# Second attention: the probability transpose moved from TensorE to DMA transposes of fp16 halves

## The reference

```python
q = _rope(_rms_norm((draft_hidden @ Wq.T).reshape(bsz, draft_len, H, HD), q_norm_w))
k = _rope(_rms_norm((kv_in @ Wk.T).reshape(bsz, total_len, KVH, HD), k_norm_w))
v = (kv_in @ Wv.T).reshape(bsz, total_len, KVH, HD)
scores = jnp.einsum('bhqd,bhkd->bhqk', q, k) * SCALE
probs = jax.nn.softmax(scores, axis=-1)
attn = jnp.einsum('bhqk,bhkd->bhqd', probs, v)
return attn.reshape(bsz, draft_len, H * HD) @ Wo.T
```

## Time and profile before

| | us |
|---|---|
| median of 3 runs | 3430.97 (3428.15 to 3434.47) |
| profiled execution | 3434.46 |
| its span | 3432.7 |
| second attention in it | 2141 to 2983 |

### The profile page before, as it was taken

One profiled execution on the slowest core, in us unless ns is written; L12 is line 12 of the kernel. 1 busy time (PEld: TensorE's weight loads), 2 busy tenths in 40 slices (PEclk: granted clock), 3 DMA queues, 4 the chain that ended last, 5 costly groups with the idle time before them and its releaser, 6 DMA issues. The chain is left out here.

```text
span 3432.7 us, 59039 instructions
## 1 busy us (share of the span) xinstructions
PE 3004.1 (88%) x17256; PEld 1779.6 (52%) x17257; DVE 1807.7 (53%) x5546; ACT 1647.5 (48%) x4343; POOL 1697.2 (49%) x2331
## 2 busy tenths in 40 slices
PE   4899999999999529999999997799999999743996
PEld 2566666665665415555555543455555555432663
DVE  4455555555555235434334444688788778521331
ACT  5777777876876213333322332455555555321332
POOL 6666666666663354454534453544444444142222
PEclk9899999999999569999999998999999999856998
DMA  6211011011010254455544565000000000117444
GB/s 234 84 53 40 31 53 40 31 53 40 31 50 31 94 198 132 143 156 153 145 141 138 153 182 140 17 21 23 18 24 18 24 18 13 50 67 287 86 84 104
DMA packets 206771, 291.78 MB, mean 85 GB/s; under 512 B 39200, under 2 KB 110368, under 8 KB 206624
## 3 DMA queue, kind: packets, MB, share of 16 engines
q1 hardware_dynamic: 143824, 211.36, 18.8%
q0 software_dynamic: 16640, 38.05, 5.5%
q10 hardware_dynamic: 46224, 41.36, 4.1%
HBM read 199.27 MB, written 95.63 MB: 86 GB/s over the span
## 5 line engine op out<-in xcount | busy, mean ns | idle before, releaser
L402 PE MATMUL a_mm<-a_w_hi,a_xq_hi 128*128 128x512 f16 x768 | 301.4, 392 | 63.8 <-POOL a_xq_lo L752 60.7
L531 DVE BATCH_NORM_STATS2 a_st<-a_mm 128x6 f32<-128x128 f32 x768 | 171.0, 285 | 323.8 <-PE a_mm L403 228.5
L633 ACT ACTIVATE a_nrm<-a_mm,a_sc_t 128x128 f32<-128x128 f32 x768 | 291.8, 478 | 99.2 <-POOL a_sc_t L770 99.0
L1530 POOL TENSOR_TENSOR e_st<-e_st,e_ws_tile 128x1024 f32<-128x1024 f32 x64 | 123.5, 1930 | 427.1 <-PE e_y L1286 416.5
L403 PE MATMUL a_mm<-a_w_hi,a_xq_lo 128*128 128x512 f16 x768 | 300.8, 392 | 0.0
L769 POOL TENSOR_TENSOR a_sc_t<-a_sc_t,a_mhalf 128x4 f32<-128x4 f32 x192 | 202.2, 1053 | 185.0 <-DVE a_sc_t L538 185.0
L1324 ACT ACTIVATE e_hh<-e_ha 128x512 f16<-128x512 f32 x128 | 76.3, 596 | 416.2 <-PE e_ha L1271 414.8
L1419 DVE SCALAR_TENSOR_TENSOR e_hl<-e_ha,e_hh 128x512 f16<-128x512 f32 x128 | 88.5, 691 | 353.8 <-ACT e_hh L1324 349.5
L1284 PE MATMUL e_y<-e_w2h,e_hh 128*128 128x512 f16 x640 | 242.6, 379 | 0.0
L1285 PE MATMUL e_y<-e_w2l,e_hh 128*128 128x512 f16 x640 | 242.6, 379 | 0.0
L1286 PE MATMUL e_y<-e_w2h,e_hl 128*128 128x512 f16 x640 | 242.6, 379 | 0.0
(11 more groups left out here) (334 smaller groups left out, 8627.7 us busy)
## 6 DMA issues: line engine op xcount, KB each, us to landing
e_st<-in_w SPq DMA_DIRECT2D x128, 512.0 KB, 4.3
disp<-a_empty SPq DMA_DIRECT2D x32, 781.5 KB, 4.9
e_st<-in_w1b SPq DMA_DIRECT2D x32, 352.0 KB, 3.1
e_xb<-disp ACTq DMA_DIRECT2D x41, 260.5 KB
e_xb<-disp SPq DMA_DIRECT2D x40, 260.5 KB, 4.4
a_cx<-in_ctxT SPq DMA_DIRECT2D x32, 256.0 KB, 3.1
a_stage<-in_wprojT SPq DMA_DIRECT2D x16, 512.0 KB, 5.0
r_xb<-x SPq DMA_DIRECT2D x32, 256.0 KB, 2.7
```

The lines of the kernel that those rows point to most:

```text
L402: pe.matmul(out, xq_hi[:, n, c, :], w_hi[:, t, c, :], start=(c == 0), stop=False)
L633: ins = act.activation(nrm[:, n % 2, i * P:(i + 1) * P], src[:, i * P:(i + 1) * P], ACT.Identity, bias=sc_t[:, n % 2, 3, i:i + 1], scale=s ...
```

## The change

The probabilities are no longer normalised in fp32 and transposed by TensorE. `row_scale` (DVE, offset 2) makes the reciprocal of the row sums times 1024. `p_high` (ACT, offset 2, first in its slot's list) writes the high half of pr times that factor, `p_low` (DVE, offset 3) the low half, both fp16 with the query still on the partition, into `pq`: 128 x 1024 for each half. `p_turn` (SP, offset 3, first in its list) issues for each half one DMA transpose from `pq` to `pT`, the first after `p_high`, the second after `p_low`. `pv` waits for both by their semaphores `turned`. The bank `PTB`, `p_transpose` and one `p_high` and one `p_low` per step go.

```diff
+        pq = [s.sb(f"pq{n}", [P, 2, 2, 4, P], F16) for n in ("h", "l")]
-        PTB = s.ps("ptb", [P, DM])
+            def p_turn(b, a, q):
+                for half, done in ((0, "phi"), (1, "plo")):
+                    sp.wait_ge(sem[done], at(a, NA1, b))
+                    if half == 0:
+                        sp.wait_ge(sem["pv"], at(a - 2, NA1, b) + 2)
+                    sp.sem_inc(sem["turning"], 1)
+                    sp.dma_start_transpose(pT[half][:, a % 2, :, :].rearrange("p c (i t) -> p (c i) t", t=P),
+                                           pq[half][:, a % 2, :, :, :].rearrange("p c i t -> p (c i t)"))\
+                      .then_inc(turned[half][a % 2], 16)
-            run_pipeline(sp, [("end", 7, store), ("end", 2, residual), ("in", 1, x_load)],
+            run_pipeline(sp, [("att", 3, p_turn), ("end", 7, store), ("end", 2, residual), ("in", 1, x_load)],
-            def p_transpose(b, a, c):
-                pe.wait_ge(sem["pnorm"], at(a, NA1, b))
-                pe.wait_ge(sem["plo"], at(2 * a + c - 1, 2 * NA1, b) + 1)
-                for i in range(4):
-                    mm = pe.transpose(PTB[:, i * P:(i + 1) * P], pr[:, a % 2, i, c * P:(c + 1) * P], ident[:])
-                mm.then_inc(sem["ptr"], 1)
             def pv(b, a, q):
-                pe.wait_ge(sem["plo"], at(2 * a + 1, 2 * NA1, b) + 1)
+                for half in range(2):
+                    pe.wait_ge(turned[half][a % 2], 16 * at(a // 2, NA1 // 2, b))
-                              ("att", 5, pv), ("att", 6, out_project),
-                              ("att", 2, lambda b, a, q: p_transpose(b, a, 0)),
-                              ("att", 3, lambda b, a, q: p_transpose(b, a, 1))], NJ1, SCORE1, None, 2)
+                              ("att", 5, pv), ("att", 6, out_project)], NJ1, SCORE1, None, 2)
-            def pnorm(b, a, q):
+            def row_scale(b, a, q):
                 dve.wait_ge(sem["exp"], at(a, NA1, b))
-                ch.link(dve.reciprocal(ri[:], rs[:]))
-                for i in range(4):
-                    p = pr[:, a % 2, i, :]
-                    ins = dve.tensor_scalar(p, p, ri[:, i:i + 1], PS, ALU.mult, ALU.mult)
-                    ch.add(ins) if i < 3 else ins.then_inc(sem["pnorm"], 1)
+                if not is0(b, a, 2):
+                    dve.wait_ge(sem["plo"], at(a - 2, NA1, b))
+                ch.link(dve.reciprocal(ri[:, a % 2, :], rs[:]))
+                dve.tensor_scalar(ri[:, a % 2, :], ri[:, a % 2, :], PS, None, ALU.mult).then_inc(sem["rinv"], 1)
+            def p_low(b, a, q):
+                dve.wait_ge(sem["phi"], at(a, NA1, b))
+                if not is0(b, a, 2):
+                    dve.wait_ge(turned[1][a % 2], 16 * at(a // 2 - 1, NA1 // 2, b))
                 for i in range(4):
+                    ins = dve.scalar_tensor_tensor(out=pq[1][:, a % 2, :, i, :],
+                                                   in0=pr[:, a % 2, i, :].rearrange("p (c t) -> p c t", c=2),
+                                                   scalar=ri[:, a % 2, i:i + 1], in1=pq[0][:, a % 2, :, i, :],
+                                                   op0=ALU.mult, op1=ALU.subtract)
-                               ("att", 3, lambda b, a, q: p_low(b, a, 0)), ("att", 4, lambda b, a, q: p_low(b, a, 1)),
-                               ("att", 2, pnorm), ("job", 0, stats), ("job", 1, v_low), ("att", 5, o_low),
+                               ("att", 3, p_low), ("att", 2, row_scale), ("job", 0, stats), ("job", 1, v_low), ("att", 5, o_low),
-            def p_high(b, a, c):
-                act.wait_ge(sem["ptr"], at(2 * a + c, 2 * NA1, b) + 1)
-                act.wait_ge(sem["pv"], at(a - 2, NA1, b) + 2)
-                act.activation(pT[0][:, a % 2, c, :], PTB[:], ACT.Copy).then_inc(sem["phi"], 1)
+            def p_high(b, a, q):
+                act.wait_ge(sem["rinv"], at(a, NA1, b))
+                if not is0(b, a, 2):
+                    act.wait_ge(turned[0][a % 2], 16 * at(a // 2 - 1, NA1 // 2, b))
+                for i in range(4):
+                    ins = act.activation(pq[0][:, a % 2, :, i, :], pr[:, a % 2, i, :].rearrange("p (c t) -> p c t", c=2),
+                                         ACT.Copy, scale=ri[:, a % 2, i:i + 1])
-            run_pipeline(act, [("att", 3, lambda b, a, q: p_high(b, a, 0)), ("att", 4, lambda b, a, q: p_high(b, a, 1)),
+            run_pipeline(act, [("att", 2, p_high),
```

More of the change, by code:

```diff
@@ L1592, in layer1_attention @@
         v = [s.sb(f"v{n}", [P, 2, 2, DM], F16) for n in ("h", "l")]
-        mx, nb, rs, ri = (s.sb(n, [P, 4], F32) for n in ("mx", "nb", "rs", "ri"))
+        mx, nb, rs = (s.sb(n, [P, 4], F32) for n in ("mx", "nb", "rs"))
+        ri = s.sb("ri", [P, 2, 4], F32)
         pr = s.sb("pr", [P, 2, 4, KEYS], F32)
+        pq = [s.sb(f"pq{n}", [P, 2, 2, 4, P], F16) for n in ("h", "l")]
         pT = [s.sb(f"p{n}", [P, 2, 2, DM], F16) for n in ("h", "l")]
@@ L1607, in layer1_attention @@
             "x_hi", "x_lo", "c_hi", "c_lo", "tabs", "mm", "stat", "scal", "rot", "rsum", "norm", "qtr", "qhi", "qlo",
-            "vhi", "vlo", "score", "max", "exp", "pnorm", "ptr", "phi", "plo", "pv", "ohi", "olo", "proj", "xres",
+            "vhi", "vlo", "score", "max", "exp", "rinv", "phi", "plo", "turning", "pv", "ohi", "olo", "proj", "xres",
             "x3", "out")}
+        turned = [[s.sem(f"turned_{n}{i}") for i in range(2)] for n in ("h", "l")]
         def at(k, per, b):
@@ L1651, in _ @@
             pe.sem_inc(sem["score"], 2)
-            pe.sem_inc(sem["ptr"], 1)
             pe.sem_inc(sem["pv"], 2)
@@ L1743, in _ @@
             dve.sem_inc(sem["olo"], 1)
-            dve.sem_inc(sem["plo"], 1)
             dve.sem_inc(sem["out"], 16)
@@ L1811, in smax @@
                 dve.tensor_scalar(nb[:], mx[:], -SCALE, None, ALU.mult).then_inc(sem["max"], 1)
-            def pnorm(b, a, q):
+            def row_scale(b, a, q):
                 dve.wait_ge(sem["exp"], at(a, NA1, b))
-                ch.link(dve.reciprocal(ri[:], rs[:]))
-                for i in range(4):
-                    p = pr[:, a % 2, i, :]
-                    ins = dve.tensor_scalar(p, p, ri[:, i:i + 1], PS, ALU.mult, ALU.mult)
-                    ch.add(ins) if i < 3 else ins.then_inc(sem["pnorm"], 1)
[L1821 to L1824, removed]
+                if not is0(b, a, 2):
[6 more added lines that the diff above has]
+                    dve.wait_ge(turned[1][a % 2], 16 * at(a // 2 - 1, NA1 // 2, b))
+                for i in range(4):
+                    ins = dve.scalar_tensor_tensor(out=pq[1][:, a % 2, :, i, :],
+                                                   in0=pr[:, a % 2, i, :].rearrange("p (c t) -> p c t", c=2),
+                                                   scalar=ri[:, a % 2, i:i + 1], in1=pq[0][:, a % 2, :, i, :],
+                                                   op0=ALU.mult, op1=ALU.subtract)
+                    ch.add(ins) if i < 3 else ins.then_inc(sem["plo"], 1)
             def o_low(b, a, q):
@@ L1904, in exps @@
                 act.wait_ge(sem["max"], at(a, NA1, b))
+                if not is0(b, a, 2):
+                    act.wait_ge(sem["plo"], at(a - 2, NA1, b))
                 if not is0(b, a, 1):
-                    act.wait_ge(sem["ptr"], at(2 * a - 3, 2 * NA1, b) + 1)
-                if not is0(b, a, 1):
-                    act.wait_ge(sem["pnorm"], at(a - 1, NA1, b))
+                    act.wait_ge(sem["rinv"], at(a - 1, NA1, b))
                 for i in range(4):
@@ L1912, in exps @@
                 ins.then_inc(sem["exp"], 1)
-            def p_high(b, a, c):
-                act.wait_ge(sem["ptr"], at(2 * a + c, 2 * NA1, b) + 1)
-                act.wait_ge(sem["pv"], at(a - 2, NA1, b) + 2)
-                act.activation(pT[0][:, a % 2, c, :], PTB[:], ACT.Copy).then_inc(sem["phi"], 1)
+            def p_high(b, a, q):
+                act.wait_ge(sem["rinv"], at(a, NA1, b))
+                if not is0(b, a, 2):
+                    act.wait_ge(turned[0][a % 2], 16 * at(a // 2 - 1, NA1 // 2, b))
+                for i in range(4):
+                    ins = act.activation(pq[0][:, a % 2, :, i, :], pr[:, a % 2, i, :].rearrange("p (c t) -> p c t", c=2),
+                                         ACT.Copy, scale=ri[:, a % 2, i:i + 1])
+                ins.then_inc(sem["phi"], 1)
             def o_high(b, a, q):
```

## The result

The changed kernel takes 3382.82 us (median of 4 runs, 3380.82 to 3385.25), beside 3429.56 us before on the same chip (4 runs): a ratio of 0.9862, 95% interval 0.9845 to 0.9879, 46.7 us less. The forecast was 3383 us. The number came true; two of the terms it was summed from did not, and the experiments are mostly about those.

The account below looks back on a forecast made before the run. The prediction took PE as the bound: -56 us from PE, +8 us for the grown gap, 0 for DVE, ACT and DMA, in sum -48 us, from 3430.97 to 3383 us; range 3365 to 3525 us.

Parts of the forecast that it names:

- What bounds the stage: Steady part: PE is the bound, with DVE (81% busy) next and the DMA engines nearly free.
- -56 us from PE: 128 blocks of four `p_transpose` at 0.44 us each leave PE, 3.5 us a batch.
- +8 us for the grown hole: PE's gap before `q_transpose` grows as PE gets there earlier, giving back 0 to 14 us, taken as 8.
- DVE at nothing: DVE's new work, 9.2 to 9.9 us a step, is hidden under PE's 11.7 us, so it costs nothing.
- The tiny multiplication: One new DVE multiplication of 128x4 in even slots, priced at 0.17 to 0.20 us like the reciprocal beside it.
- a lost cover: If DVE's idle time before `o_low` in odd slots no longer hid `p_low`: at most 0.7 us a step, 45 us.
- ACT at nothing: ACT's four new `p_high` and their wait for `rinv` cost nothing; 0 to 1.4 us a step if not in time.
- The turns at nothing: The two transposing DMAs of a step land after 4.5 us each, hidden before `pv` with 10 and 16 us of room.
- The rival: The turning queue becomes the bound once two turns exceed 12.6 us a step: 3521 or 3971 us, chance 0.22.
- The two pages: Trainium skill pages on DMA transposes: one gives an estimated 10.5 us a turn, the other 1.0 us; rows decide neither.
- The ends: Last steps without jobs, where two turns replace transposes, `p_high` and `p_low`: taken as nothing, -3 to +5 us.

Follow-up runs that it names:

- the new order: `q_low` and `x_low` put ahead of `o_low` in DVE's list: 3360.02 us in the changed kernel, 3411.91 us in the kernel before.

## Why the forecast was right, point by point

**What bounds the stage: half right.** I read PE as the bound, with 1.5 us of holes a batch that would grow to some 2.0. In fact PE's list (48.1 us of work a batch before, 44.6 after, by the distances between starts) is tied to the chain stats, scales, normalise, exps, `o_high`, `o_low`, `q_low` over DVE, POOL and ACT; that the tie runs through `o_low` and `q_low` is shown by the new order, the rest of the chain is read from the kernel's waits. With PE's work as before, the rest of the change alone gives 1.19 us a batch; and 4.0 us of DVE work a batch, added where the old weight stood, undo the whole gain (51.04 us, in a run with 3.7 us more DVE time a batch than before). DVE's busy share of 81% misled me: most of its idle time lies in front of `o_low` (109.6 us in 13.3 batches are 8.2 us of the 9.6 it is idle in one), where it waits and can't use it.

**-56 us from PE: the work went, the price was too high.** Put back alone, the same PE work cost 28 us. Only with the hole before `q_transpose` closed is it worth 3.38 of its 3.5 us a batch.

**+8 us for the grown hole: right by its net, wrong by its parts.** By the stores the holes grew by 3.5 - 3.11 = 0.4 us a batch, 6 us in 16 (PE's recorded waits say 0.7, 11 us). Behind this stand a growth of 1.6 us a batch by PE's lead (3.5 - 1.92) and a shrinking of 1.2 with the rest of the change. The forecast had the growth at 0.9 and named the shrinking ("`stats` starts up to 1.4 us earlier"), but charged it to a hole and not as a gain on which the rest depends. The sum came out at 48 us, measured 46.7, because two errors offset each other: 28 us too much for PE's work, and some 19 us (1.19 x 16) left out for what the rest of the change gives. That the number is so close is luck.

**DVE at nothing: right as it stands, wrong as a claim of room.** Four instructions of `p_low` take 1.67 us merged in three steps of four, in my 1.1 to 1.8, and 2.5 us in the fourth, outside it. The tiny multiplication, priced at 0.17 to 0.20 us, has a mean of 0.41. The price I gave for a lost cover, at most 0.7 us a step, came from the idle time of the odd slot; in the even slot 0.4 us more a step cost 15 us and 1.0 us cost 55.

**ACT at nothing: right.** `p_high` takes 1.70 us merged (1.4 to 1.9 forecast); its wait of 129.6 us for `rinv` is the largest of ACT's, and moving it away gained 0.1 us a batch.

**The turns at nothing: right.** They land after 3.0 us (4.5 taken, 2.1 to 12.6 allowed) and hold the engines for 1.3 to 1.5 us, under the whole of the range (2.4 to 10.5). A packet of a turn costs 22 ns, under the 37 ns of the cheapest row I had the earlier trace rows. The room before `pv` is at least 7.2 us after the landing, so 10.2 from the issue, as forecast. The rival stood at 12.6 us of turns a step (it should have been the new step's 11.8); there were 2.7 to 3.0, and the runs put the limit at 8 turns, 11.9 us.

**The two pages.** The estimate of 10.5 us a turn that follows from 1309 ns for a 128x128 block (the Trainium skill, VectorE: DVE Perf Modes, "The three transpose paths") is refuted by this trace for eight blocks in one DMA: 3.0 us to landing. The 261 GB/s of the Trainium skill's page DMA: Bandwidth & Descriptors are nearer, though not reached here: 256 KB in 1.48 us are 177 GB/s, and with the plain loads and stores between the turns the full queue moved 194 GB/s.

**The ends.** I had -3 to +5 us. The last three intervals each got 2.6 to 3.2 us shorter, like any batch, so the turns hardly showed there. But the room is nearly gone: in the last four steps the low half lands 0.2 to 1.8 us before its `pv`, and one `pv` waits for it.

```profile
2907.99 1.23 SPq L1653 DMA_TRANSPOSE a_pl<-a_pql  x1
...
2913.01 0.38 PE L1670 MATMUL a_ovb<-a_ph,a_vh 128*128 128x512 f16 x1 [0.37 <-DMA a_pl<-a_pql]
```

With 6 us more the ends cost 18 us, which I had not foreseen.

## What to carry to other kernels

When a bounding engine has small holes that end with another engine's step, treat the two as tied: first find what makes the hole (here the order of DVE's list, worth 23 us by itself), and only then price a microsecond of either engine. DVE's busy share of 81 to 84% said nothing about its room in the slot that counted; put weight on an engine in the slot in question and measure. Turning fp16 halves by DMA cost nothing here, where 10 us lie between issue and reading and the queue is nearly idle; count the issuing engine's 1.24 us for each, and look at the last steps, where the distance shrinks.

## What the runs showed of the hardware

- A DMA transpose of 128x1024 fp16 from SBUF to SBUF, issued by SP, takes 1.23 to 1.24 us to issue and lands after 3.0 us. With the queue full a turn comes every 1.48 to 1.49 us (32 in 47.74 us, 40 in 59.08, the plain loads and stores among them), each takes 1.33 us to issue, and its landing still reads 3.2 to 3.4 us.
- A multiplication of 128x4 on DVE takes 0.17 us in most places and 1.15 in others: in 2250 to 2880 us the reciprocal of the same shape has a mean of 168 ns, and the multiplication right behind it 411. Of the 42 in 2300 to 2800 us, the ten long ones start 0.14 us after an instruction of POOL on `a_r`, 128x512 (1.27 us), and end 0.03 us after it; none of the 32 short ones overlaps one. No run moved one of the two away, so the cause is read from this and not tested.

```profile
L1821 DVE TENSOR_SCALAR a_ri<-a_ri 128x4 f32<-128x4 f32 x53 | 21.8, 411 | 1.8
...
L1820 DVE RECIPROCAL a_ri<-a_rs 128x4 f32<-128x4 f32 x53 | 8.9, 168 | 0.0
...
2625.16 1.27 POOL L1990 TENSOR_TENSOR a_r<-a_r 128x512 f32<-128x512 f32 x1
2625.30 1.16 DVE L1821 TENSOR_SCALAR a_ri<-a_ri 128x4 f32<-128x4 f32 x1
```
